# Degree sums over a ring of 14 one-hot groups with one signal in seven, and self rows turned two tiles to a bank

## What is computed

```python
def gcn_conv(x, src, dst, w, W, b, n):
    xw = x @ W
    deg = jax.ops.segment_sum(w, dst, num_segments=n)
    dinv = jnp.where(deg > 0, jax.lax.rsqrt(deg), 0.0)
    norm = dinv[src] * w * dinv[dst]
    out = jax.ops.segment_sum(xw[src] * norm[:, None], dst, num_segments=n)
    return out + b
# every node also has an edge to itself of weight 1
out = relu(gcn_conv(layernorm(x), ..., W1, b1, n))
out = gcn_conv(out, ..., W2, b2, n)
out = relu(batchnorm(out) * gamma + beta + layernorm(x))
x = x + out
x = x + top2_of_8_experts(layernorm(x))     # 256 -> 512 -> 256, gelu
```

## Time and profile before

| | us |
|---|---|
| median of the timed runs | 3007.58 (3001.88 to 3009.61, 3 runs) |
| the profiled execution | 2998.0 |
| its span, first to last instruction | 2996.2 |
| TensorE busy, matmul | 2110.1 (70%) |
| GpSimd busy | 1639.9 (55%) |
| VectorE busy | 903.2 (30%) |
| ScalarE busy | 378.4 (13%) |

### The profile page before, as it was taken

How to read it: one execution, slowest core, us unless ns; L and a number is a source line. 1 busy time by engine, 2 the same in 40 slices (tenths; PEclk the granted TensorE clock), 3 DMA queues, 4 the chain that set the end, 5 groups by cost and what they waited for, 6 DMA issues and landing times.

```text
span 2996.2 us, 34126 instructions
## 1 busy us (share of the span) xinstructions
PE 2110.1 (70%) x10594; PEld 1505.7 (50%) x10595; DVE 903.2 (30%) x2713; ACT 378.4 (13%) x1053; POOL 1639.9 (55%) x1732
## 2 busy tenths in 40 slices
PE   0000055997887886776588888788888467999987
PEld 0000043444554555565455555555555353888886
DVE  8400065012121222333222222322222775333332
ACT  7000001000000000000000000000000461343333
POOL 1777703016666666666466666565655320666665
PEclk9999999999998998777789998898988655999999
DMA  9950005545554553333455454454444522777775
GB/s 332 320 173 1 0 0 160 161 135 151 153 159 140 161 153 90 119 114 103 127 159 156 143 156 142 136 153 144 146 139 118 179 87 101 176 190 186 182 185 126
DMA packets 264400, 431.32 MB, mean 144 GB/s; under 512 B 39664, under 2 KB 147887, under 8 KB 264143
## 3 DMA queue, kind: packets, MB, share of 16 engines
q1 hardware_dynamic: 181455, 253.80, 26.7%
q0 software_dynamic: 81088, 173.80, 22.6%
q10 hardware_dynamic: 1728, 2.13, 0.2%
HBM read 339.36 MB, written 91.16 MB: 144 GB/s over the span
## 4 chain that ended last, share of the span: by engine, by line
PE 43%; another core or an unknown queue 23%; DVE 13%; issue 11%; DMA 6%; POOL 3%; POOLq 1%; DVEq 1%; ACT 1%; SPq 0%; ACTq 0%
PE psum L1391 17%; PE psum L1406 13%; DMA ACC<-rows_for_experts,ACC 4%; PE psum L1355 3%; DVE arena L1008 3%; PE psum L1510 2%; PE psum L1518 2%; POOL out_dram L589 2%; PE psum L1485 2%; PE psum L1344 1%; DMA out_dram<-ACC 1%; DVE ACC L884 1%; PE psum L1310 1%; PE psum L1501 1%
## 5 line engine op out<-in xcount | busy, mean ns | idle before, releaser
L533 POOL DMA_INDIRECT arena<-conv_rows,edge_cols x1120 | 1062.6, 949 | 876.8 <-issue 318.2
L1391 PE MATMUL psum<-arena,X 128*128 128x512 f32 x1568 | 811.2, 646 | 93.2 <-issue 49.5
L1406 PEld LDWEIGHTS psum<-arena 128*128 128x128 f32 x4480 | 629.0, 207 | 390.1 <-issue 380.1
L1406 PE MATMUL psum<-arena 128*128 128x128 f32 x4480 | 663.5, 293 | 202.8 <-issue 189.5
L1391 PEld LDWEIGHTS psum<-arena,X 128*128 128x128 f32 x1568 | 297.6, 206 | 359.2 <-issue 314.4
L1032 DVE TENSOR_TENSOR ACC<-ACC,psum 128x256 f32 x80 | 33.8, 422 | 906.7 <-remote 613.9
L520 POOL DMA_INDIRECT pair_weights<-scale_b,mean_b x224 | 227.3, 1015 | 135.6 <-issue 68.0
L1008 DVE TENSOR_SCALAR arena<-iota,edge_cols 128x128 f32<-128x128 f32 x1120 | 294.5, 368 | 0.4 <-DVE ACC L940 0.2
L1310 PE MATMUL psum<-ACC 128*128 128x6 bf16 x784 | 56.1, 202 | 326.5 <-DVE ACC L884 202.3
L1310 PEld LDWEIGHTS psum<-ACC 128*128 128x128 bf16 x784 | 51.4, 158 | 331.2 <-DVE ACC L884 206.5
L1510 PE MATMUL psum<-ACC,arena 128*128 128x128 f32 x1680 | 208.3, 277 | 0.2 <-DVE ACC L1241 0.2
(11 more groups left out here) (277 smaller groups left out, 1368.1 us busy)
## 6 DMA issues: line engine op xcount, KB each, us to landing
arena<-pair_weights SPq DMA_DIRECT2D x392, 256.0 KB
arena<-in_L_ffn_W_dram SPq DMA_DIRECT2D x113, 512.0 KB, 7.9
pair_weights<-zeros SPq DMA_DIRECT2D x4, 12544.0 KB, 42.7
arena<-conv_rows,edge_cols POOLq DMA_INDIRECT x1120
conv_rows<-X SPq DMA_DIRECT2D x14, 896.0 KB
X<-in_x_dram SPq DMA_DIRECT2D x12, 896.0 KB, 10.4
rows_for_experts<-ACC SPq DMA_DIRECT2D x7, 910.0 KB, 4.2
out_dram<-X SPq DMA_DIRECT2D x6, 896.0 KB
```

The costliest lines, as they stand in the source:

```text
L533: pool.indirect_dma_start(G[:, n * D:(n + 1) * D], None, y_tab[layer], bass.IndirectOffsetOnAxis(srcT[:, t:t + 1], 0)).then_inc(gathered[n ...
L1391: ins = m.matmul(bank(6 + c, BW), X[:, t * D + c * P:t * D + (c + 1) * P], A_in[:, u * BW:(u + 1) * BW], start=(t == 0), stop=(t == NT - 1))
L1406: ins = m.matmul(bank(2 * (k % 2) + c, P), G[:, n * D + c * P:n * D + (c + 1) * P], S[:, n * P:(n + 1) * P], start=(j == 0), stop=(j == GT ...
```

## The change

DQ = 7 is new. The degree loop has four rounds of two halves with seven groups each. lob has 14 one-hot groups and lies in the arena; w_group has 14 groups of weights. VectorE waits for oh_free once in a half, copies 42 sums at once, and then builds seven groups, each raising lob_ready. TensorE waits for lob_ready for each group, writes group r of a half into six columns of its bank of its own, and raises oh_free behind the seventh. The operations of a group are the same.

The self rows of layer 0 go two tiles to a bank over banks 2 to 5. VectorE copies two tiles with one operation; TensorE raises self_turned by two behind the second tile, and waits in self_added for the pair four before. Layer 1's self rows are as before.

```diff
-        lob = early(2 * GT * P, BF16)
+        lob = arena[:, 0:DQ * GT * P].bitcast(BF16)
...
-        w_group = early(2 * 6 * GT, BF16)
-        sums = w_rest[:, 0:6 * (NG + 2)]
+        w_group = early(2 * DQ * 6 * GT, BF16)
+        sums = w_rest[:, 0:6 * (NG + 2 * DQ)]
...
-                    with dve.Fori(0, NG // 2) as i:
+                    with dve.Fori(0, NG // (2 * DQ)) as i:
                         for h in range(2):
                             dve.wait_ge(oh_free, i * 2 + (h + 1))
-                            v.tensor_copy(sums[:, bass.ds(i * 12 + h * 6, 6)], bank(2 + h, 6))
-                            v.tensor_copy(w_group[:, h * 6 * GT:(h + 1) * 6 * GT],
-                                          w_split[:, bass.ds(i * (12 * GT) + h * 6 * GT, 6 * GT)])
...
+                            v.tensor_copy(sums[:, bass.ds(i * (12 * DQ) + h * 6 * DQ, 6 * DQ)], bank(2 + h, 6 * DQ))
+                            for q in range(h * DQ, (h + 1) * DQ):
+                                v.tensor_copy(w_group[:, q * 6 * GT:(q + 1) * 6 * GT],
+                                              w_split[:, bass.ds(i * (12 * DQ * GT) + q * 6 * GT, 6 * GT)])
+                                v.tensor_tensor(lob[:, q * GT * P:(q + 1) * GT * P].rearrange("p (n t) -> p n t", t=GT),
...
+                                                    [P, P, GT]), ALU.is_equal).then_inc(lob_ready, 1)
-                    dve.wait_ge(oh_free, 2 + NG)
+                    dve.wait_ge(oh_free, 2 + NG // DQ)
...
                     if layer == 0:
-                        for t in range(NT):
-                            take_self(0, t, t, 4)
+                        for t in range(0, NT, 2):
+                            m = min(2, NT - t)
+                            dve.wait_ge(self_turned, t + m)
+                            v.tensor_copy(acc[:, :, t * P:(t + m) * P].rearrange("p c (t n) -> p c t n", n=P),
+                                          bank(2 + t // 2 % 4, m * D).rearrange("p (t c n) -> p c t n", c=KC, n=P)
+                                          ).then_inc(self_added, m)
...
+                            for r in range(DQ):
+                                q = h * DQ + r
+                                pe.wait_ge(lob_ready, i * (2 * DQ) + (q + 1))
+                                hot = lob[:, q * GT * P:(q + 1) * GT * P].rearrange("p (n t) -> p n t", t=GT)
+                                for j in range(GT):
+                                    ins = m.matmul(bank(2 + h, 6 * DQ)[:, r * 6:(r + 1) * 6], hot[:, :, j],
+                                                   w_group[:, (q * GT + j) * 6:(q * GT + j + 1) * 6],
+                                                   start=(j == 0), stop=(j == GT - 1))
                             ins.then_inc(oh_free, 1)
...
+                            if t >= 8 and t % 2 == 0:
+                                pe.wait_ge(self_added, t - 6)
+                            for k in range(KC):
+                                ins = m.transpose(bank(2 + t // 2 % 4, 2 * D)[:, t % 2 * D + k * P:t % 2 * D + (k + 1) * P],
+                                                  X[:, t * D + k * P:t * D + (k + 1) * P], ident[:, :])
+                            if t % 2 or t == NT - 1:
+                                ins.then_inc(self_turned, 1 + t % 2)
```

More of the change, by code:

```diff
@@ L22 @@
 MAXIN = 40
+DQ = 7
 KEY = 8192
@@ L82, in gnn_ffn @@
     GG = NG - DG
+    assert NG % (2 * DQ) == 0 and DQ * GT * P <= 2 * GT * D + 2 * GT * P + ASLOTS * BG * P
     RH = HALO + RW + HALO
@@ L888, in _ @@
-                    dve.wait_ge(oh_free, 2 + NG)
+                            v.tensor_copy(sums[:, bass.ds(i * (12 * DQ) + h * 6 * DQ, 6 * DQ)], bank(2 + h, 6 * DQ))
[3 more added lines that the diff above has]
+                                v.tensor_tensor(lob[:, q * GT * P:(q + 1) * GT * P].rearrange("p (n t) -> p n t", t=GT),
+                                                iota_b.rearrange("p (n t) -> p n t", t=GT),
+                                                lo_b[:, bass.ds(i * (2 * DQ * GT) + q * GT, GT)].unsqueeze(1).broadcast_to(
+                                                    [P, P, GT]), ALU.is_equal).then_inc(lob_ready, 1)
@@ L889, in _ @@
+                    dve.wait_ge(oh_free, 2 + NG // DQ)
                     for h in range(2):
-                        ins = v.tensor_copy(sums[:, 6 * (NG + h):6 * (NG + h + 1)], bank(2 + h, 6))
+                        ins = v.tensor_copy(sums[:, 6 * (NG + h * DQ):6 * (NG + (h + 1) * DQ)], bank(2 + h, 6 * DQ))
                     chain_fast(ins)
-                    v.tensor_reduce(deg_cols, sums[:, 12:6 * (NG + 2)].rearrange("p (g k) -> p g k", k=3), AX_X,
+                    v.tensor_reduce(deg_cols, sums[:, 12 * DQ:6 * (NG + 2 * DQ)].rearrange("p (g k) -> p g k", k=3), AX_X,
@@ L1303, in _ @@
                 with pe.If(general == 0):
-                    with pe.Fori(0, NG // 2) as i:
+                    with pe.Fori(0, NG // (2 * DQ)) as i:
                         for h in range(2):
-                            pe.wait_ge(lob_ready, i * 2 + (h + 1))
-                            hot = lob[:, h * GT * P:(h + 1) * GT * P].rearrange("p (n t) -> p n t", t=GT)
-                            for j in range(GT):
-                                ins = m.matmul(bank(2 + h, 6), hot[:, :, j],
-                                               w_group[:, (h * GT + j) * 6:(h * GT + j + 1) * 6],
-                                               start=(j == 0), stop=(j == GT - 1))
+                            for r in range(DQ):
[6 more added lines that the diff above has]
+                                                   start=(j == 0), stop=(j == GT - 1))
                             ins.then_inc(oh_free, 1)
@@ L1334, in turn_self @@
                 def turn_self(layer, n, t, b):
[L1335 to L1340 removed]
+                    pe.wait_ge(y_ready, n + 1)
                     if n >= 2:
@@ L1379, in aggregate @@
                         for t in range(NT):
-                            turn_self(0, t, t, 4)
+                            c, j = divmod(t, CH)
+                            pe.wait_ge(y0_dve, Y_DVE * c + min(j + 1, Y_DVE))
+                            pe.wait_ge(y0_act, (CH - Y_DVE) * c + max(j + 1 - Y_DVE, 0))
+                            if t >= 8 and t % 2 == 0:
[5 more added lines that the diff above has]
+                                ins.then_inc(self_turned, 1 + t % 2)
                     pe.wait_ge(self_added, NT * (layer + 1))
```

10 lines of the change are left out of this document (removed).

## The result

The changed kernel takes 2926.44 us (2919.82 to 2933.57, 4 runs), the kernel before, on the same chip and in the same rounds, 3004.73 (2997.76 to 3009.61, 4 runs): a ratio of 0.974, with the 95% interval from 0.9705 to 0.9771. The profiled execution took 2933.57 us, its span is 2931.8. All lines behind the degree loop have moved in the code: L881 is L883 now, L884 is L887, L890 is L893, L934 is L937.

What follows compares the result with a forecast made beforehand. It took TensorE signals held during GpSimd's bursts, delaying the degree loop ahead of y0 and then the self rows, as the bound. 17 us from the degree loop plus 11 from the self rows, off 3007.6, gave 2980; range 2955 to 3005.

Steps and rivals of the forecast that it cites:

- What bounds the kernel, what the delay counts: Degree loop and self rows: TensorE's signals come late during GpSimd's bursts, by instructions in front, 1.40 us each in a long burst.
- TensorE is done at 119: Degree loop: TensorE finishes the first 14 groups at 119 us, though their signals reach VectorE much later.
- signals: Rival, chance 0.12: the delay is per signal, so the degree loop ends at 400 and 82 us are gained, 2926.
- Part one: Degree loop: 48 of 56 signals and copies of sums removed, loop end at 440.6, 17.0 us earlier.
- the curve of delay against the burst's age: Delay per TensorE instruction grows with the age of GpSimd's burst, from 0.2 us at first to 1.40 in the long burst.
- VectorE builds 14 groups without a wait, to about 118: Degree loop: starting at 102.06 as before, VectorE builds the first 14 groups of one-hots before it must wait for signal 1.
- The pace of 1.14 us a group: Degree loop: VectorE's time for a group in the new loop, 1.30 before, bounds 1.10 and 1.30.
- The rival on code: Rival, chance 0.07: TensorE's 392-instruction loop body is fetched again on each return, making the kernel slower, 3020 at 20 us each.
- Part two: Self rows: the dense products start 24.5 us earlier, of which 11 stay because dense loads starve near unit 15.
- Dense starts at T + 28: T is the start of y0; the dense products start 28 us behind it instead of 52.5.
- After the dense head all moves as one block: Behind the first dense units, the groups of gathers and sums and the FFN shift together, keeping the 28 us.

Runs made afterwards that it cites:

- a signal for each group: The changed kernel, but TensorE raises oh_free behind every group, 56 signals instead of 8: 2929.54 us (one run).
- the ring alone: Only the new degree loop put into the kernel before, self rows still one tile to a bank over two banks: 2920.39 us, ratio 0.975.
- short one-hots: The changed kernel, but from group 15 on VectorE writes only 14 of the 1792 elements of a group's one-hots: 2962.64 us (one run).
- pause kernel: The changed kernel, but GpSimd stops its scatter after 56 transfers until VectorE has copied the last self row: 2952.04 us, 0.9674 of the kernel before.
- the pause and useless work together: The changed kernel with GpSimd's scatter stopped for the self rows and 128 useless two-input VectorE operations, a small copy ahead of each: 2883.74 us, ratio 0.9508.
- a ring of four groups: The changed kernel with DQ = 2, 28 signals: 3000.80 us (one run), on a chip where the kernel before takes 3052.38.

## Why the prediction was wrong

- *What bounds the kernel, what the delay counts.* Right as to the count. The 1.40 us an instruction showed as 39.2 (28 instructions), 5.60 (4) and 11.20 (8, self rows and dense units alike). Not right was that TensorE runs as far ahead as it likes ("TensorE is done at 119", with 392 instructions out): where the delay is, it gets some 62 instructions ahead and then stands itself. I gave signals a chance of 0.12, and that rival's number, 2926, is the time measured, by accident: of its steps the loop's end at 400 came out as 166, and its cause is refuted by three runs (a signal for each group, the ring alone, short one-hots).
- *Part one, the step that failed.* I took it that the delay is there whenever GpSimd issues, put signal 1 at 272, signals 2 and 3 at 399.5 and the loop's end at 440.6, and worked out 17 us. No signal was waited for, and the loop ended at 166.28, because VectorE's unbroken one-hots slowed GpSimd to 1.97 us a transfer. I read the curve of delay against the burst's age and didn't ask what sets the burst's pace. The timeline of GpSimd in the kernel before held a hint, one row ahead of 100.87, the start of the full pace in the earlier trace rows:

```profile
98.27 2.30 POOL L520 DMA_INDIRECT pair_weights<-scale_b,mean_b  x1 [0.30 <-issue]
```

  2.30 us (since 84.54) while VectorE ran two-input operations in the opening (L868 and L871, from 84.10 to 100), 0.95 behind them. "VectorE builds 14 groups without a wait, to about 118" is the sentence where I should have asked what this does to GpSimd. In place of the 17 us: 291 us at y0.
- *The pace of 1.14 us a group* was 1.12. TensorE's long loop body showed no idle time of its own: 0.20 us ahead of the half at 119.41, which starts the body again, and it waits there for VectorE. The rival on code falls.
- *Part two, a second step that failed.* "Dense starts at T + 28" was T + 236 in the whole change, since the loop's early end puts the self rows into the scatter. By itself 20.6 us behind y0, where I had 11: its dense start was right (24.7 against 28 us), the starving over-sized, 4.7 us where I had 14. In the whole change it brought nothing that shows: the pairs take 11.2 us there, and the ring alone was as fast.
- *"After the dense head all moves as one block".* Right: 76 us at the first block's end and at the first group's sum, 78 in the medians.
- *Where the gain went.* 291 us at y0, 184 of it lost in the self rows (236 us from y0's start to the dense start, against 52), 31 more in the dense head, which starves beside the gathers. The pause kernel shows that only 21 of these could be had back by order alone; the pause and useless work together get back 80. That the total, 78, is only 2.8 times the forecast and not ten times is the sum of two large errors of opposite sign.

## What to carry to other kernels

Two engines can set each other's pace, as VectorE's two-input operations and GpSimd's transfers do here, so a change that makes one of them wait less also changes what the other does to a third: ask of a removed wait not only who runs earlier but who is slowed down by it. Where a delay was seen under one load, look in the same trace for the load under which it was absent before you carry it to the new schedule. When a signal is late, look whether its sender stands too. And count what a signal stands behind from the trace, weight loads too, each time anew. A gain can also belong to the chip: this one comes out of a delay that one chip here doesn't have.

## What the runs showed of the hardware

- On every chip here but one, TensorE's instructions pass at one in 1.40 us while GpSimd issues indirect transfers back to back at 1.26 us. With up to some 60 of them out, TensorE looks quick and only its signals are late (39.2 us behind 28 instructions); with more it stands itself (2.80 us for a weight load and a matmul in the short one-hots, 189.5 us in the groups of the kernel before). Some 27 us behind a long burst what is held is let go. At 1.97 us a transfer on average there is no delay, at 1.42 about half of it. On one chip it isn't there at 1.26 us either, and the kernel before takes 2480 us instead of 3001 to 3055. What in the chip differs, and by what path GpSimd slows TensorE, no run here shows.
- The state seems to feed itself: a ring of four groups ran freely for eleven halves (24 us) and then fell into the delay, with waits of 3.5, 6.3, 50 and 75 us.
- VectorE's two-input bfloat16 operations of 1.08 us stretch a GpSimd transfer from 0.96 to 1.9 us with a small copy between them and to 1.70 us without. Twice one transfer was held as long as a whole row of 96 operations (96 us beside two-input ones, 52 beside float32 copies from SBUF to SBUF), and twice, in the second rows of the same traces, none was. One-input scaling of y0 hardly stretches one (0.96 to 1.04).
